# The two-way scan layer in 1024-column chunks, one channel tile at a stage, odd states' input built by ScalarE in turned form

## Chip, cores and metric

The kernel runs on one core of a Trainium2 chip. The metric is device time in microseconds (us) of one execution of the whole program, the median of several runs. The engines are TensorE (PE, its weight loads PEld), VectorE (DVE), ScalarE (ACT), GpSimd (POOL) and SyncE (SP), which issues the DMAs.

## What is computed

Four layers run one after the other on `x` of shape (4, 128, 64, 64): sparse attention, a selective scan with 64 states, rank-one attention, and a selective scan in both directions with 16 states. The change rewrites the last one:

```python
def _mamba(xf, Win, conv_w, conv_b, Wx, Wdt, bdt, A_log, D, Wout):   # xf: (1, 16384, 128)
    u, z = split(xf @ Win.T, 2)                   # 256 inner channels each
    u = silu(causal_conv(u, conv_w, taps=4) + conv_b)
    dt, Bm, Cm = split(u @ Wx.T, [8, 16, 16])
    delta = softplus(dt @ Wdt.T + bdt)
    A = -exp(A_log)                               # (256, 16)
    h[l] = exp(delta[l] * A) * h[l-1] + delta[l] * Bm[l] * u[l]    # for each of 256 x 16
    y[l] = sum_n h[l, :, n] * Cm[l, n] + u[l] * D
    return (y * silu(z)) @ Wout.T
y = _mamba(x) + flip(_mamba(flip(x)))             # both directions over 16384 positions
out = silu(group_norm(y, 4 groups)) + x
```

## The kernel before

`network` calls the four layers in turn; `xp` holds `x` with three columns of padding on both sides in SBUF, through all four. Layer 3, `two_way_scan_layer`, is the one that the change touches. It has 256 channels, two tiles (e = 0, 1) of 128, and 16 states (n), so 32 units for each chunk of `CH` = 512 columns. There are 32 chunks forward (d = 0) and 32 backward (d = 1). Each engine runs `chunks(engine, body)`: hardware loops over two chunks, with the work of a chunk K and the preparation of chunk K+1 woven in by constant positions (`N_BC`, `N_DELTA`, n or s). There is no scheduler: an engine's order is the order of the code, and semaphores tie the engines together.

For one unit s = 2n + e of chunk K: PE copies the row of B to all partitions (`broadcasts`, L1415, once for both e, a bfloat16 product with one-hot rows on three-part split values); DVE multiplies it with `du` = delta*u (`state_input`, L1623, into PSUM); ACT makes `decay` = exp(delta*A) (`decays`, L1523) and before it saves the last column of an old state (L1522, `carry`); DVE runs the recurrence (`scan`, L1631); POOL multiplies the state with C, whose row a DMA has spread over the partitions (L1573, `c_row`); PE adds the product into `y_sum` with the identity (`add_state`, L1423). The preparation of a chunk: four convolution taps folded into the input weights (`prep_u`, L1378), `prep_z` (L1387), B, C and dt (`prep_bc`, L1394), delta (`prep_delta`, L1406), softplus in steps on ACT (L1504 to L1510) and DVE (`soft_a` to `soft_d`, L1600 to L1614), the bfloat16 splits on ACT and DVE (L1587, L1593), `input_rate` on POOL (L1563). Its result: `gating` on DVE (L1639, L1643), `project` (L1430), `result` (L1649, L1652, L1654). A last part normalises and adds `x` (L1760, L1789) in eight pieces of 2048 columns.

Layer 1, `scan_layer`, is not changed, but it is a second, differently built scan in the same profile. It takes 1024 columns at a time and its states in pairs P: an even state gets its input as above (broadcast L642, product on DVE L1004); for the odd one ACT scales 128x128 blocks of the transposed `du` by a column of B (`odd_input`, L810), and PE turns them back into PSUM (`turn_back`, L652), from where the scan reads. The other lines there are `decays` L797, `scan` L1017, `keep` L1023, `product` L906 on POOL, `add_state` L662, `soft_round` L975 and `soft_max` L979 on DVE.

## Time and profile before

| | us |
|---|---|
| median of 3 runs | 11610.69 (11608.76 to 11611.1) |
| the profiled execution, own time | 11606.67 |
| its span | 11604.9 |
| layer 1, first input product to the last scans | 2986 to 6177 |
| layer 3, first input product to the last scan | 7213 to 11536 |
| layer 3, last part (affine, silu, skip) | 11553 to 11605 |

The page gives busy time by engine for the whole program, a mean of four layers with different limits. So a layer is read by a view of its own stretch: the busy time and granted TensorE clock of a window, then the timeline of single instructions inside. Where two instructions of an engine follow without idle time, start minus start is what one costs its engine; the duration of one is a little longer, since the next starts before it ends.

### The profile page before, as it was taken

To read this page: it belongs to the slowest core of one execution; us is meant where nothing else is said; L and a number is where in the kernel's file an instruction comes from. 1 tells how busy PE (TensorE), PEld (TensorE's weight loads), DVE (VectorE), ACT (ScalarE), POOL (GpSimd) and SP (SyncE) were. 2 spreads that over 40 slices of the span, in tenths; PEclk is the share of its full clock that TensorE was granted. 3 is DMA by queue.
4 is the path that set the end of the run, shared out by engine and by line. 5 is a ranking of instruction groups with operands and counts; after the bars stand their busy time and mean duration, and the time that the engine had idled before them with its cause. 6 is when DMAs were issued, how large, how long until landed. Compare 5 with 4: busy or idle time off the path is not lost. (4 is left out here: it accounts for less than half of the span.)

```text
span 11604.9 us, 133673 instructions
## 1 busy us (share of the span) xinstructions
PE 10299.4 (89%) x37124; PEld 5447.6 (47%) x37124; DVE 9629.0 (83%) x10210; ACT 7224.1 (62%) x13486; POOL 5495.9 (47%) x3348
## 2 busy tenths in 40 slices
PE   9999999999899999999999999778778777777775
PEld 6767777677444444444444454333333333322332
DVE  6858668587799999999993122999999999999998
ACT  5636556365688888888885545555555555555554
POOL 0000000000578888887882000666666666666665
PEclk9999989899899999999999999888888888898897
DMA  0000000000355455455451000222222222222223
GB/s 37 0 1 0 0 0 0 0 0 0 128 169 170 171 168 171 169 171 170 170 175 48 0 0 13 67 66 69 67 66 67 69 69 70 72 70 69 70 72 112
DMA packets 317319, 872.87 MB, mean 75 GB/s; under 512 B 35985, under 2 KB 36113, under 8 KB 314257
## 3 DMA queue, kind: packets, MB, share of 16 engines
q1 hardware_dynamic: 316912, 868.43, 23.0%
q8 instruction: 136, 2.23, 0.1%
q14 instruction: 271, 2.21, 0.1%
HBM read 834.73 MB, written 33.55 MB: 75 GB/s over the span
## 5 line engine op out<-in xcount | busy, mean ns | idle before, releaser
L1573 POOL TENSOR_TENSOR l_ring<-l_ring 128x512 f32<-128x512 f32 x2048 | 2678.6, 1329 | 1332.8 <-DVE l_ring L1631 818.1
L906 POOL TENSOR_TENSOR l_hc<-l_h,l_hc 128x1024 f32<-128x1024 f32 x1024 | 2412.1, 2377 | 613.8 <-DVE l_h L1017 613.3
L1423 PE MATMUL l_ps<-l_ring,w_sb 128*128 128x512 f32 x4096 | 2273.8, 681 | 371.8 <-DVE l_gated L1639 308.7
L1631 DVE TENSOR_TENSOR_SCAN l_ring<-l_ring,l_carry,l_ps 128x512 f32<-128x512 f32 x2048 | 2524.9, 1263 | 0.0
L662 PE MATMUL l_ps<-l_hc,w_sb 128*128 128x512 f32 x4096 | 1947.3, 597 | 32.7 <-POOL l_hc L906 27.0
L1017 DVE TENSOR_TENSOR_SCAN l_h<-l_decay,l_carry,l_ps 128x1024 f32<-128x1024 f32 x768 | 1759.3, 2332 | 3.7 <-PE l_ps L652 0.2
L1523 ACT ACTIVATE l_ring<-l_delta,w_sb 128x512 f32<-128x512 f32 x2048 | 1444.8, 708 | 48.4 <-DVE l_ring L1631 33.0
L1423 PEld LDWEIGHTS l_ps<-l_ring,w_sb 128*128 128x128 f32 x4096 | 845.8, 213 | 1224.1 <-issue 983.9
L114 POOL COPY l_qm<-l_q 128x128 f32 x128 | 82.3, 645 | 2728.2 <-PE l_ps L175 2331.0
L797 ACT ACTIVATE l_decay<-l_delta,w_sb 128x1024 f32<-128x1024 f32 x1024 | 1161.6, 1139 | 285.5 <-DVE l_h L1017 284.3
L1623 DVE TENSOR_TENSOR l_ps<-l_du,l_ps 128x512 f32<-128x512 f32 x2048 | 1299.4, 678 | 27.3 <-DVE l_ring L1631 18.4
L810 ACT ACTIVATE l_xt<-l_duT,l_BT 128x128 f32<-128x128 f32 x4096 | 1246.1, 387 | 0.0
L199 PE MATMUL l_ps<-l_attnT,l_vT 128*128 128x128 f32 x8192 | 1112.5, 279 | 1.7 <-ACT l_attnT L267 1.7
L175 PE MATMUL l_ps<-l_k,l_qm 128*128 128x512 f32 x2048 | 1023.9, 603 | 25.0 <-DVE l_E L370 18.9
L662 PEld LDWEIGHTS l_ps<-l_hc,w_sb 128*128 128x128 f32 x4096 | 741.4, 191 | 624.9 <-issue 498.8
L199 PEld LDWEIGHTS l_ps<-l_attnT,l_vT 128*128 128x128 f32 x8192 | 994.6, 192 | 47.0 <-ACT l_attnT L267 43.2
L1522 ACT ACTIVATE l_carry<-l_ring 128x1 f32<-128x1 f32 x1984 | 376.6, 190 | 1025.0 <-DVE l_delta L1614 778.0
L1415 PE MATMUL l_ps<-l_stack,sel 96*128 96x512 bf16 x1024 | 415.5, 406 | 576.8 <-DVE l_ps L1623 573.7
L1159 PE MATMUL l_ps<-l_E,l_hs 128*128 128x512 f32 x2048 | 880.0, 592 | 5.2 <-DVE l_hs L1225 5.2
L376 DVE SCALAR_TENSOR_TENSOR l_E<-l_relu,l_E 128x1024 f32<-128x1024 f32 x512 | 626.3, 1224 | 287.4 <-ACT l_E L260 287.4
L260 ACT ACTIVATE l_E<-l_E,l_offsets 128x1024 f32<-128x1024 f32 x512 | 587.0, 1147 | 290.8 <-DVE l_E L370 290.8
L370 DVE TENSOR_TENSOR l_E<-l_relu,l_ps 128x1024 f32<-128x1024 f32 x512 | 624.9, 1221 | 138.8 <-ACT l_relu L254 138.2
(222 smaller groups left out, 13282.6 us busy)
## 6 DMA issues: line engine op xcount, KB each, us to landing
l_hc<-l_rows_dram SPq DMA_DIRECT2D x1024, 512.0 KB, 3.7
l_ring<-l_rows_dram SPq DMA_DIRECT2D x1024, 256.0 KB, 3.2
l_recon_dram<-l_recon SPq DMA_DIRECT2D x64, 256.0 KB, 3.4
l_loaded<-l_recon_dram SPq DMA_DIRECT2D x32, 256.0 KB, 3.5
l_ring<-l_recon_dram SPq DMA_DIRECT2D x8, 1024.0 KB, 7.0
out<-l_ring SPq DMA_DIRECT2D x8, 1024.0 KB, 4.9
xp<-x_in SPq DMA_DIRECT2D x1, 6144.0 KB, 23.8
l_rows_dram<-l_z SPq DMA_DIRECT2D x16, 256.0 KB, 4.4
```

Source lines behind the costliest of these rows:

```text
L175: ins = nc.tensor.matmul(logits[c % 2][:, j * BANK:(j + 1) * BANK], qm[:, h, :], k[:, c * CH + j * BANK:c * CH + (j + 1) * BANK], start=Tr ...
L199: ins = nc.tensor.matmul(ps[:, 7 - h, 0:128], vT[:, t * 128:(t + 1) * 128], attnT[:, g % 2, j * 128:(j + 1) * 128], start=t == 0, stop=t = ...
L662: ins = nc.tensor.matmul(y_sum[:, half(j)], ident, hc[:, unit % CS, half(j)], start=q == 0, stop=q == S1 - 1)
L797: nc.scalar.activation(decay[:, unit % DS, :], delta[:, p, :], ACT.Exp, scale=wt("A")[:, q:q + 1]).then_inc(decay_ready, 1)
L810: ins = nc.scalar.activation(xt[:, (2 * P + hf) % XS, t * 128:(t + 1) * 128], duT[:, p, blk, :], ACT.Identity, scale=BT[:, p, blk, k:k + 1])
L906: nc.gpsimd.tensor_tensor(hc[:, unit % CS, :], h[:, unit % HS, :], hc[:, unit % CS, :], ALU.mult).then_inc(hc_done, 1)
L1017: nc.vector.tensor_tensor_scan(h[:, unit % HS, :], decay[:, unit % DS, :], odd_in if odd else even_in, before, ALU.mult, ALU.add).then_inc ...
L1423: nc.tensor.matmul(y_sum[:, e, :], ident, hc[:, (n * TI + e) % 4, :], start=n == 0, stop=n == S3 - 1).then_inc(sum_mm, 1)
L1523: nc.scalar.activation(decay[:, s % DS, :], delta[:, p, e, :], ACT.Exp, scale=col("A", e * S3 + n)).then_inc(decay_ready, 1)
L1573: nc.gpsimd.tensor_tensor(hc[:, s % 4, :], h[:, s % DS, :], c_row[:, n % CS, :], ALU.mult)\
L1623: nc.vector.tensor_tensor(x_in[:, s % 2, :], du[:, p, s % TI, :], b_psum[:, s // TI % 2, :], ALU.mult)\
L1631: nc.vector.tensor_tensor_scan(h[:, s % DS, order], decay[:, s % DS, order], x_in[:, s % 2, order], carry[:, s:s + 1], ALU.mult, ALU.add). ...
```

## The change

Layer 3 is rewritten after the pattern of layer 1. Chunks have 1024 columns, 16 forward and 16 backward. A *stage* S is one chunk K and one channel tile e: 64 stages with 16 states in 8 pairs r = 0 to 7, 512 pairs P in all. The code of all stages is written out, without hardware loops. The even state's input stays on PE and DVE (`broadcast_B`, `even_input`); the odd state's is made by ACT (`odd_input`, eight instructions) and turned back by PE (`turn_back`, eight transposes), for which PE transposes `du` (`turn_du`) and the odd rows of B (`turn_B`). The saved column of a state goes from ACT to DVE (`keep`, two small copies for a pair). POOL takes two steps of softplus, the gating, and both subtractions of the split. z and the gate are computed in the forward direction alone, kept in DRAM (`gate_dram`), and loaded in the backward one. `x` is stored to DRAM by layer 2 and loaded in windows `xw`; so the last part loads `x` too. The C rows are loaded straight into the slots `hc`, five of them, and multiplied in place. The weights of layer 3 are loaded at its start, not during layer 2. Semaphores of layer 0 are cleared and used again.

```diff
 def rank_one_attention_layer(...):
         def _(sp):
-            for to, at, signal in loads:
-                sp.dma_start(to, at).then_inc(signal, 16)
+            for b in range(B):
+                for j in range(0, NB, 2):
+                    sp.wait_ge(bank_free, NB + b * NB + j + 2)
+                    at = slice(b * N + j * BANK, b * N + (j + 2) * BANK)
+                    sp.dma_start(x_dram[:, at], x[:, at]).then_inc(x_stored, 16)
...
 def two_way_scan_layer(...):
-    CH = BANK
+    CH = 1024
...
 @block.tensor
+            def turn_back(P):
+                at_least(pe, scan_done, 2 * P)
+                for hf in range(2):
+                    pe.wait_ge(xt_ready, 2 * P + hf + 1)
+                    for t in range(4):
+                        ins = nc.tensor.transpose(odd_bank(hf)[:, t * 128:(t + 1) * 128],
+                                                  xt[:, (2 * P + hf) % XS, t * 128:(t + 1) * 128], ident)
+                    ins.then_inc(xt_mm, 1)
+            def pieces(S, r):
+                    if r == 0 and more:
+                        for j in range(2):
+                            project_delta(S + 1, j)
+                    if r == 1 and e == 1 and K + 1 < NK:
+                        turn_B(K + 1)
+                    if r in (1, 2) and n < 4 * NK:
+                        conv(n, [2 * r - 2, 2 * r - 1])
+                    if r == 2 and forward(K):
+                        project_z(S, 0)
+                    if r in (3, 4) and n < 4 * NK:
+                        conv(n + 1, [2 * r - 6, 2 * r - 5])
+                    if r == 4 and forward(K):
+                        project_z(S, 1)
+                    if r == 5 and more:
+                        turn_du(S + 1, 0)
+                        turn_du(S + 1, 1)
+                    if r in (6, 7) and e == 0 and K + 1 < NK:
+                        project_bc(K + 1, r - 6)
+                    if r in (6, 7) and e == 1 and K:
+                        project_out(K - 1, r - 6)
+                for P in range(NS * PAIRS):
+                    turn_back(P)
+                    if P:
+                        add_state(2 * P - 2)
+                    pieces(*divmod(P, PAIRS))
+                    if P + 1 < NS * PAIRS:
+                        broadcast_B(P + 1)
+                    if P:
+                        add_state(2 * P - 1)
...
 @block.scalar
+            def pieces(S, r):
+                    if r == 0 and more:
+                        for j in range(2):
+                            delta_copy(S + 1, j)
+                    if r == 1 and more:
+                        soft_exp(S + 1)
+                    if r == 2 and forward(K):
+                        silu_u(n)
+                        silu_z(S, 0)
+                        exp_set()
+                    if r == 4 and forward(K):
+                        silu_u(n + 1)
+                        silu_z(S, 1)
+                        exp_set()
+                for P in range(NS * PAIRS):
+                        decays(2 * P + 2)
+                        odd_input(P + 1)
+                        decays(2 * P + 3)
+                    pieces(*divmod(P, PAIRS))
...
 @block.gpsimd
+                for P in range(NS * PAIRS):
+                    product(2 * P)
+                    product(2 * P + 1)
+                    if r == 1 and S:
+                        gating(S - 1)
+                    if S % TI == 1 and S // TI + 1 < NK:
+                        if r == 1:
+                            split_rest(S // TI + 1)
+                        if r == 5:
+                            split_last(S // TI + 1)
+                    if S + 1 < NS:
+                        if r == 2:
+                            soft_low(S + 1)
+                        if r == 3:
+                            soft_sum(S + 1)
+                        if r == 4:
+                            input_rate(S + 1)
...
 @block.vector
+                for P in range(NS * PAIRS):
+                    scan(P, 0)
+                    scan(P, 1)
+                    if r == 0 and S:
+                        add_y(S - 1)
+                    if P + 1 < NS * PAIRS:
+                        even_input(P + 1)
+                    if S // TI % NCH < NCH - 1:
+                        keep(2 * P)
+                        keep(2 * P + 1)
+                    pieces(S, r)
...
 @block.sync
             def _(sp):
+                def load(i):
+                    sp.dma_start(buf[:, i % 2, :], recon_dram[:, at]).then_inc(buf_in[i % 2], 16)
+                    sp.dma_start(skip[:, i % 2, :], x_dram[:, at]).then_inc(buf_in[i % 2], 16)
```

On PE, in the loop over chunks, before: a broadcast and two state sums for two 512-column units (one n, both tiles), then a tap.

```order
2949 L1378 MATMUL l_ps<-xp,l_taps 128x512
2950 L1415 MATMUL l_ps<-l_stack,sel 128x512
2951 L1422 REGISTER_ALU
2952 L1423 MATMUL l_ps<-l_ring,w_sb 128x512
2953 L1422 REGISTER_ALU
2954 L1423 MATMUL l_ps<-l_ring,w_sb 128x512
```

On PE now, in a forward stage, pairs 1 (from its `turn_B`) and 2; L1496 is `turn_back`, L1506 `add_state`, L1486 `broadcast_B`, L1435 a convolution tap, L1443 z.

```order
3541 L1456 MATMUL l_ps<-w_sb,l_rest 128x32 x8
3542 L1435 MATMUL l_ps<-l_xw,l_taps 128x512 x2
3543 L1486 MATMUL l_ps<-l_stack,sel 128x512 x2
3544 L1506 MATMUL l_ps<-l_ring,w_sb 128x512 x2
3545 L1496 MATMUL l_ps<-w_sb,l_xt 128x128 x8
3546 L1506 MATMUL l_ps<-l_ring,w_sb 128x512 x2
3547 L1435 MATMUL l_ps<-l_xw,l_taps 128x512 x2
3548 L1443 MATMUL l_ps<-l_xw,w_sb 128x512
```

What moved: every pair of states now carries eight transposes, and preparation stands in each of the eight places of a stage.

On POOL before, where `input_rate` of the next chunk (L1563) stands among the products (L1573):

```order
182 L1563 TENSOR_TENSOR l_du<-l_delta,l_u 128x1024
183 L1573 TENSOR_TENSOR l_ring<-l_ring 128x512 x4
```

On POOL now, in a stage with e = 1, pairs 1 to 5 (products are L1786; `gating` L1781, `split_rest` L1751, `soft_low` L1760, `soft_sum` L1765, `input_rate` L1771, `split_last` L1755):

```order
480 L1781 TENSOR_TENSOR l_yg<-l_yg,l_gate 128x1024
481 L1751 TENSOR_TENSOR l_rest<-l_rest,l_part 96x1024
482 L1786 TENSOR_TENSOR l_ring<-l_ring 128x1024 x2
483 L1760 TENSOR_TENSOR l_z<-l_z 128x1024
484 L1786 TENSOR_TENSOR l_ring<-l_ring 128x1024 x2
485 L1765 TENSOR_TENSOR l_delta<-l_delta,l_z 128x1024
486 L1786 TENSOR_TENSOR l_ring<-l_ring 128x1024 x2
487 L1771 TENSOR_TENSOR l_du<-l_delta,l_u 128x1024
488 L1786 TENSOR_TENSOR l_ring<-l_ring 128x1024 x2
489 L1755 TENSOR_TENSOR l_stack<-l_rest,l_part 96x1024
```

What moved: one extra instruction behind the two products of a pair became one in each of pairs 1 to 4, two in pair 1 of every second stage.

## Rows read from the trace of the kernel before

**Rows 1.** The page: span; busy time and share of the span by engine
```profile
span 11604.9 us, 133673 instructions
PE 10299.4 (89%) x37124; PEld 5447.6 (47%) x37124; DVE 9629.0 (83%) x10210; ACT 7224.1 (62%) x13486; POOL 5495.9 (47%) x3348
```
**Rows 2.** Windows: busy time by engine and granted clock, layer 1 and layer 3
```profile
core 0: us, PE busy (x) PEld busy (x) DVE busy (x) ACT busy (x) POOL busy (x), PEclk, DMA share, GB/s
2986.00:6177.00 3191.00, 3014.38 (x10930) 1513.78 (x10930) 3154.60 (x2562) 2588.76 (x5501) 2576.98 (x1100) 0.99 0.50 169
7213.00:11536.00 4323.00, 3378.87 (x7118) 1344.36 (x7118) 4273.93 (x4758) 2402.81 (x5100) 2822.95 (x2111) 0.88 0.23 69
```
**Rows 3.** Lines L1631, L1623: count, ns min/median/max, first and last start
```profile
L1631 DVE TENSOR_TENSOR_SCAN l_ring<-l_ring,l_carry,l_ps x2048: 1242/1266/1280, 7214.2 to 11534.6; 128x512 f32<-128x512 f32 x187
L1623 DVE TENSOR_TENSOR l_ps<-l_du,l_ps x2048: 661/680/697, 7213.0 to 11532.9; 128x512 f32<-128x512 f32 x187
```
**Rows 4.** Timeline of DVE in layer 1: start, duration, instruction, count
```profile
4598.01 4.58 DVE L1017 TENSOR_TENSOR_SCAN l_h<-l_decay,l_zero,l_ps 128x1024 f32<-128x1024 f32 x2
4602.50 1.21 DVE L1004 TENSOR_TENSOR l_ps<-l_du,l_ps 128x1024 f32<-128x1024 f32 x1
4603.62 0.21 DVE L1023 COPY l_carry<-l_h 128x1 f32<-128x1 f32 x2
4603.75 4.58 DVE L1017 TENSOR_TENSOR_SCAN l_h<-l_decay,l_zero,l_ps 128x1024 f32<-128x1024 f32 x2
```
**Rows 5.** Timeline of PE in layer 1, the same place
```profile
4600.41 0.60 PE L642 MATMUL l_ps<-l_stack,sel 96*128 96x512 bf16 x2 [1.34 <-DVE l_h L1017]
4600.85 1.88 PE L662 MATMUL l_ps<-l_hc,w_sb 128*128 128x512 f32 x4
4602.64 1.09 PE L652 MATMUL l_ps<-w_sb,l_xt 128*128 128x128 f32 x8
4603.57 1.88 PE L662 MATMUL l_ps<-l_hc,w_sb 128*128 128x512 f32 x4
4605.29 1.02 PE L618 MATMUL l_ps<-xp,l_taps 128*128 128x512 f32 x2
4606.15 0.60 PE L642 MATMUL l_ps<-l_stack,sel 96*128 96x512 bf16 x2
```
**Rows 6.** Timelines of POOL and DVE in layer 1, around its softplus steps
```profile
4607.57 9.28 POOL L906 TENSOR_TENSOR l_hc<-l_h,l_hc 128x1024 f32<-128x1024 f32 x4
...
5908.52 5.65 POOL L906 TENSOR_TENSOR l_hc<-l_h,l_hc 128x1024 f32<-128x1024 f32 x2
...
5897.15 2.00 DVE L975 TENSOR_SCALAR l_usq<-l_z 128x1024 f32<-128x1024 f32 x1
...
5910.53 1.42 DVE L979 SCALAR_TENSOR_TENSOR l_delta<-l_delta,l_z 128x1024 f32<-128x1024 f32 x1
```
**Rows 7.** Timeline of ACT in layer 1: two decays, eight odd inputs
```profile
4599.30 2.23 ACT L797 ACTIVATE l_decay<-l_delta,w_sb 128x1024 f32<-128x1024 f32 x2
4601.44 2.43 ACT L810 ACTIVATE l_xt<-l_duT,l_BT 128x128 f32<-128x128 f32 x8
```
**Rows 8.** Timeline of ACT at the start of layer 3: a table load
```profile
7204.55 1.06 ACT L1506 ACTIVATE l_z<-l_z 128x1024 f32<-128x1024 f32 x1
7205.67 1.28 ACT L1510 ACT_TABLE_LOAD   x1
```
**Rows 9.** PE in layer 3 after a wait, and the window of that stretch
```profile
8434.68 3.64 PE L1423 MATMUL l_ps<-l_ring,w_sb 128*128 128x512 f32 x4 [3.97 <-DVE l_gated L1639]
...
8434.60:8438.20 3.60, 3.52 (x5) 1.56 (x6) 3.56 (x5) 1.97 (x2) 1.27 (x1) 0.53 0.04 16
```
**Rows 10.** ACT in the last part; landing time of its 1 MB loads (page)
```profile
11554.50 4.08 ACT L1760 ACTIVATE l_ring<-l_ring,l_shift,l_scale 128x2048 f32<-128x2048 f32 x2
...
11596.14 2.09 ACT L1760 ACTIVATE l_ring<-l_ring,l_shift,l_scale 128x2048 f32<-128x2048 f32 x1 [3.00 <-DMA l_ring<-l_recon_dram]
...
l_ring<-l_recon_dram SPq DMA_DIRECT2D x8, 1024.0 KB, 7.0
```

More of the change, by code:

```diff
@@ L1325, in two_way_scan_layer, with place, keeps_before, _ @@
+        def place(K):
+            d, c = divmod(K, NCH)
+            return (NCH - 1 - c) * CH if d else c * CH
+        forward = lambda K: K < NCH
+        def keeps_before(P):
+            d, i = divmod(P, NCH * TI * PAIRS)
+            kept_pairs = (NCH - 1) * TI * PAIRS
+            return 2 * (d * kept_pairs + min(i, kept_pairs))
+        with nc.Block() as block:
+            @block.gpsimd
+            def _(pool):
+                pool.sem_clear(retired)
         with nc.Block() as block:
@@ L1493, in split_again @@
-                def split_again(K):
-                    act.wait_ge(rest_ready, K + 1)
-                    nc.scalar.activation(part[:], rest[:], ACT.Copy).then_inc(middle, 1)
-                def deltas(K, p):
-                    for e in range(TI):
-                        act.wait_ge(delta_mm, K * TI + e + 1)
-                        nc.scalar.activation(delta[:, p, e, :], [even, odd][e], ACT.Identity,
-                                             bias=col("dtr_b", e)).then_inc(delta_out, 1)
-                    act.drain()
-                    nc.scalar.activation(z1[:], delta[:, p, :, :], ACT.Abs)
-                    act.drain()
-                    nc.scalar.activation(z1[:], z1[:], ACT.Exp, scale=-1.0).then_inc(exp_ready, 1)
@@ new lines, in _ @@
+                for j in range(2):
+                    rest_copy(0, j)
+                split_high(0)
+                split_middle(0)
+                for j in range(2):
+                    delta_copy(0, j)
+                exp_set()
+                soft_exp(0)
+                soft_log(0)
+                for n in (4, 5):
+                    silu_u(n)
+                exp_set()
+                for j in range(2):
+                    duT_copy(0, j)
+                decays(0)
+                odd_input(0)
@@ new lines, in soft_round, with soft_max @@
+                def soft_round(T):
+                    dve.wait_ge(exp_ln, 2 * T + 1)
+                    nc.vector.tensor_scalar(z3[:], z1[:], 1.0, 1.0, ALU.add, ALU.subtract).then_inc(soft_steps, 1)
+                def soft_max(T):
+                    dve.wait_ge(exp_ln, 2 * T + 2)
+                    own = delta[:, T % 2, :]
+                    nc.vector.scalar_tensor_tensor(out=own, in0=own, scalar=0.0, in1=z2[:], op0=ALU.max,
+                                                   op1=ALU.add).then_inc(soft_steps, 1)
@@ new lines, in keep, with pieces @@
+                def keep(unit):
+                    S, q = divmod(unit, S3)
+                    K, e = divmod(S, TI)
+                    at = CH - 1 if forward(K) else 0
+                    dve.wait_ge(scan_done, unit + 1)
+                    nc.vector.tensor_copy(carry[:, e * S3 + q:e * S3 + q + 1], h[:, unit % HS, at:at + 1]).then_inc(kept, 1)
+                def pieces(S, r):
+                    K, e = divmod(S, TI)
+                    if e == 1 and K + 1 < NK:
+                        if r == 1:
+                            bt_copy(K + 1)
+                    if S + 1 < NS:
+                        if r == 2:
+                            soft_round(S + 1)
+                        if r == 3:
+                            soft_max(S + 1)
+                    if r in (6, 7) and e == 1 and K and not forward(K - 1):
+                        result(K - 1, r - 6)
+                    if r == 3 and S == (NCH - 2) * TI:
+                        dve.wait_ge(z_mm, 4 * (NCH - 3) + 4)
+                        nc.vector.memset(xw[:, NCH % 3, CH:CH + PAD], 0.0).then_inc(pad_ready, 1)
@@ L1707, in _ @@
[L1707 to L1709 removed]
+                bt_copy(0)
+                soft_round(0)
+                soft_max(0)
+                even_input(0)
+                for P in range(NS * PAIRS):
+                    S, r = divmod(P, PAIRS)
+                    scan(P, 0)
+                    scan(P, 1)
+                    if r == 0 and S:
+                        add_y(S - 1)
+                    if P + 1 < NS * PAIRS:
+                        even_input(P + 1)
[3 more added lines that the diff above has]
+                    pieces(S, r)
```

872 lines of the change are left out of this document (466 added, 406 removed).

## The prediction

> **What bounds the kernel now.** I read the page first: PE is busy 89% of the span, but that is a mean of four layers [rows 1]. So I take layer 3's own window next. There DVE is busy 4273.9 of 4323 us, PE 3378.9, POOL 2823.0, ACT 2402.8, at a granted clock of 0.88 [rows 2]. DVE is the bound, and waits for nobody: 2048 scans and 2048 input products lie end to end from 7213.0 to the last scan's end near 11536 [rows 3]. A 1024-column pair of states costs four times (1.18 + 0.59) = 7.1 us there; softplus, splits, gating and results make the rest.
>
> Layer 1 is the pattern that layer 3 shall follow, with the same 1024 scans of 1024 columns. It took 3191 us, again DVE bound (3154.6 busy), at clock 0.99, with PE at 94% and ACT and POOL at 81% [rows 2]. The question is whether layer 3 gets layer 1's time or is stopped by PE or POOL, which have more to prepare: a stage has 8 pairs to hide it, layer 1's chunk had 32.
>
> **Demand of each engine for a stage.** Starts minus starts:
>
> - DVE: a pair is two scans (4.49), the even product (1.12) and two copies (0.13), 5.74 in all: 4603.75 - 4598.01 [rows 4]. Eight make 45.9. To this come `soft_round` 2.00 and `soft_max` 1.42 [rows 6], `add_y` about 1.2 (one SBUF and one PSUM input, as the even product), `bt_copy`, and in the backward direction two result pieces of about 1.4 in every second stage. 50.6 us forward, some 52 backward.
> - PE: a pair is the broadcast 0.44, two state sums of 1.79 and 1.72, the eight transposes 0.93: 4.88; a 128x512 float32 product costs 0.86 (4606.15 - 4605.29) [rows 5]. Eight pairs make 39.0. Preparation of a stage: 8 taps, 2 delta products, 2 (4 in every second) of `project_bc` or `project_out`, counted per stage as 4 in two adjoining places, `turn_du` 0.93, and z twice forward. That is r0 1.72, r1 1.72, r2 2.58, r3 1.72, r4 2.58, r5 0.93, r6 and r7 1.72: 14.7 us forward, 13.0 backward, and 0.9 for `turn_B` with e = 1. So 54.2 forward and 52.5 backward: above DVE. The delta product, with 8 rows, is counted like the others.
> - POOL: a product is 2.33 us (9.28 for four) [rows 6]. Sixteen, the three softplus and rate steps and the gating make 46.6; with e = 1 the two subtractions of the split make 51.3, if they cost 2.33 too. No row has a bfloat16 input on POOL; I bound them by half and twice the product, 1.2 and 4.7, and take the product's value since the count of columns is the same.
> - ACT: a pair is two decays 2.14 and the odd input 2.34 or so [rows 7], 4.5 in all, 36 for a stage. Forward preparation is ten activations of 0.6 to 1.06 and four table loads of 1.28 (5.1): 14.5, and 2.1 more for the splits: 50.3 and 52.5 us. Backward it is two loads and no z: 47.
>
> The table load has its own row: the activation before it ends at 7205.61, the load starts at 7205.67 and is over 1.28 later [rows 8]. The Trainium skill (ScalarE: Activation LUTs, What ACT_TABLE_LOAD costs) gives 1.283 us and a drain of 1.38 for every switch. By that a forward stage of ACT would be 56 to 58 us and about 60 us would be added over 32 stages. The trace shows no drain here; I stay with the row.
>
> **The path in a stage.** All four engines lie within 10% of each other, so the order decides. In r6, r7 and r0 PE is last: 4.88 + 1.72 = 6.6 each. In r0 `add_y` waits for the last state sum, at the end of PE's place. It is done 1.3 us into r1; the first state sum of the new stage waits half a microsecond for it; then DVE makes the even product and the first scan, which ends 4.9 us into r1. From there **POOL** has one chain without a gap: pairs 1 to 4 hold 8 products and 4 preparation steps, 12 operations of 2.33 = 28.0, with e = 1 13 operations = 30.3. Its last is `input_rate`, and the very next place, r5, has `turn_du` on PE waiting for it. One product in that stretch is held up by `soft_max`: two took 5.65 instead of 4.67 beside it [rows 6], so +1.0. After it PE has the transposes 0.93, the broadcast 0.44 and a state sum 1.72: 3.1.
>
> Stage = 6.6 + 4.9 + 28.0 + 1.0 + 3.1 + 2 x 6.6 = **56.8 us**, with e = 1 **59.1**. Against it PE alone has 54.2 or less: PE stands 2 to 5 us at r5. Queued behind that wait are the broadcast for pair 6 and a state sum, so DVE waits too; nobody else has work to fill it. ACT, a pair ahead, isn't late anywhere in this sum, though in r2 to r4 forward only by about a microsecond.
>
> A wait of 3.97 us before L1423 was followed by 3.6 us at half clock: four records took 3.47 instead of 1.72 [rows 9]. The waits of layer 1 end at 2.3 us or so, and its clock was 0.99. With e = 1 the wait is 3.5 to 5 us, so I add 2.0 to these stages. Mean (56.8 + 61.1)/2 = 58.9; 64 stages = **3772 us**, against 4323.
>
> **Around the loop.** Ahead: layer 2's last store, then 1.3 MB of weights and the first window, which no longer load under layer 2; 1 MB lands in 7.0 us [rows 10]. The first chunk's preparation is twice as wide. Before, it took from 7181 to 7213, 32 us. I take +29 (bounds +15 and +60, the whole preparation doubled and the loads in a row). The drain of the last stage has 1024-wide steps: +6 (0 to 12). The last part moved 16.8 MB in 41.6 us for seven of eight pieces, ACT waiting for the loads [rows 10]; half as much again for `x` is +25 (0 if latency set it, 30). Stores of x, z and recon lie beside work, on SP's queue between C loads, which have some 4 us in hand: POOL reaches a product 8 us after PE frees its slot, and a C row lands in about 4. If that cover fails, a product waits and the POOL chain grows by as much; nothing in the trace lets me exclude 1 us a stage. Reused semaphores cost one short block. Layers 0 to 2 don't change.
>
> Sum: 11606.7 - 4323 + 3772 + 60 = 11115.4; the profiled execution lies 4 below the median: **11120 us**, ratio 0.958.
>
> **Rivals.**
>
> 1. *PE alone sets the end.* POOL catches up (split steps at 1.2, `soft_max` harmless, gating early). Then a stage is PE's 54.2 or 52.5 and 0.6 for the `add_y` wait, 53.9: 11120 - 64 x 5.0 = 10800. For it: POOL's demand is below PE's. Against: the twelve operations in a row, at 2.33, can't be shortened by anything in the code.
> 2. *More waits, or the clock.* The clock stays at the 0.88 of layer 3 before [rows 2], since PE again waits once or twice a stage. PE's 53.4 become 60.7, with 3 us of POOL wait left 63.7: 64 x 63.7 = 4077, 11425. Hops between engines that I set at nothing lead to the same side: 0.1 us in each of 24 is 2.4 a stage, 11270. For it: all engines tie. Against: layer 1 held 0.99 at the same share of PE. The Trainium skill (TensorE: Matmul & The Clock Gate, Part 4: PE-mode transpose) says that transposes don't count as PE activity for the clock; the change adds over seventy to a stage. By that rule the clock would sink as in this rival. The trace disagrees: layer 1's pairs have the same eight transposes and ran at 0.99 [rows 2, 5].
> 3. *Slower.* One mechanism: half clock lasts. It decides when a stage exceeds (4323 - 60)/64 = 66.6 us, that is a mean clock under 53.4/66.6 = 0.80 on PE. At 0.75 a stage is 71.2: 11606.7 - 4323 + 4557 + 60 = 11901. Before, with PE only 78% busy, it was still 0.88, which speaks against.
> 4. *It isn't done as said*: layer 3 stays DVE bound, as layer 1: 50.6 to 52 us a stage, 3285, 10630. PE's demand excludes it, unless products are cheaper than 0.86.
>
> **Numbers.** My sum, stages of 56 to 60.5 us (10930 to 11220): 0.55. Rival 1: 0.12. Rival 2, 11220 to 11500: 0.26. Rival 3: 0.04. Rival 4: 0.03. The range goes from 10880 (stage 55.2) to 11360 (62.7), which leaves out most of rivals 1, 3 and 4 and the end of 2. A measurement tells 0.2% (23 us) from no change. Faster 0.95, within 0.2% 0.01, slower 0.04.
>
> **What would show it.** DVE in layer 3 idle for some 8 us a stage, most of it before the even product and behind PE. PE waiting for `du` from POOL once a stage, 2 to 3 us with e = 0 and 4 to 5 with e = 1, and at half clock just after the latter. POOL without a gap from pair 1 to pair 4. Forward and backward stages alike (if backward is 1.7 us shorter, PE set it). The last part near 77 us instead of 52. I am wrong if PE waits for ACT's copies of the two preparation banks, if POOL waits for C rows, or if the POOL chain has gaps.

## The result, and the profile of the changed kernel

The changed kernel takes **11139.74 us** (11137.64 to 11143.06, four runs) beside 11610.9 (11608.76 to 11612.1): ratio 0.9594, 95% interval 0.9579 to 0.961. The forecast was 11120 us. The profiled execution has a span of 11139.1 us, 465.8 less than the 11604.9 of before.

The page of the changed kernel, span and busy time by engine, answering to [rows 1]:

```profile
span 11139.1 us, 128149 instructions
PE 10416.8 (94%) x41860; PEld 5841.7 (52%) x41860; DVE 8778.3 (79%) x8226; ACT 7929.4 (71%) x14477; POOL 5817.0 (52%) x2580
```

Windows of layer 3's loop, whole, forward and backward (columns as in [rows 2]: window, its us, busy time and count of PE, PEld, DVE, ACT, POOL, granted clock, DMA share, GB/s):

```profile
7245.00:11055.00 3810.00, 3479.34 (x11808) 1729.84 (x11806) 3416.17 (x2775) 3098.46 (x6074) 3131.29 (x1337) 0.98 0.48 161
...
7245.00:9150.00 1905.00, 1769.55 (x5999) 878.18 (x5998) 1697.24 (x1360) 1629.44 (x3136) 1561.36 (x670) 0.98 0.47 158
9150.00:11055.00 1905.00, 1709.79 (x5810) 851.65 (x5808) 1718.93 (x1416) 1469.02 (x2939) 1569.93 (x667) 0.98 0.49 163
```

DVE was busy 99% of the layer's loop before and is busy 90% now; PE went from 78% to 91%, POOL from 65% to 82%, and the clock from 0.88 to 0.98. No engine is full. The loop, from its first even product (7238.06) to the end of its last scan (11050.85), is 3812.8 us, 59.6 us a stage. Forward and backward take nearly the same time (1909 and 1902 us from scan to scan), though PE has less to do backward: PE doesn't set the end alone.

Waits of the changed kernel between 7260 and 11000 (engine and line, what it waited for, us in total, times, longest):

```profile
POOL l_ring L1786 <- DVE l_ring L1868: 588.1, 222, 4.9
DVE l_ps L1852 <- PE l_ps L1486: 247.8, 203, 4.2
...
PE l_ps L1469 <- POOL l_du L1771: 147.2, 63, 2.7
...
DVE l_yg L1836 <- PE l_ps L1506: 131.2, 62, 2.6
```

The third row is the wait that the forecast put in pair 5: once in each stage, 2.3 us on average. In the same stretch POOL waits for no DMA, and PE for nothing of ACT's. One whole stage with e = 1 shows how it comes about. Timeline of POOL (start, duration, line, operation; in brackets the idle time before it and what ended it):

```profile
8140.19 4.69 POOL L1786 TENSOR_TENSOR l_ring<-l_ring 128x1024 f32<-128x1024 f32 x2 [4.93 <-DVE l_ring L1868]
8144.83 2.38 POOL L1781 TENSOR_TENSOR l_yg<-l_yg,l_gate 128x1024 f32<-128x1024 f32 x1
8147.15 2.15 POOL L1751 TENSOR_TENSOR l_rest<-l_rest,l_part 96x1024 f32<-96x1024 f32 x1
8149.24 4.68 POOL L1786 TENSOR_TENSOR l_ring<-l_ring 128x1024 f32<-128x1024 f32 x2
8154.56 2.34 POOL L1760 TENSOR_TENSOR l_z<-l_z 128x1024 f32<-128x1024 f32 x1 [0.63 <-DVE l_z L1823]
8156.88 4.69 POOL L1786 TENSOR_TENSOR l_ring<-l_ring 128x1024 f32<-128x1024 f32 x2
8162.73 2.35 POOL L1765 TENSOR_TENSOR l_delta<-l_delta,l_z 128x1024 f32<-128x1024 f32 x1 [1.16 <-DVE l_delta L1828]
8165.05 4.68 POOL L1786 TENSOR_TENSOR l_ring<-l_ring 128x1024 f32<-128x1024 f32 x2
8169.69 2.35 POOL L1771 TENSOR_TENSOR l_du<-l_delta,l_u 128x1024 f32<-128x1024 f32 x1
```

Thirteen operations from the first scan of the new stage to du, and two gaps (0.63 and 1.16), each ended by one of DVE's softplus steps. The timeline of DVE at the same place:

```profile
8135.24 1.28 DVE L1836 SCALAR_TENSOR_TENSOR l_yg<-l_u,w_sb,l_ps 128x1024 f32<-128x1024 f32 x1 [2.56 <-PE l_ps L1506]
...
8150.14 4.34 DVE L1823 TENSOR_SCALAR l_z<-l_z 128x1024 f32<-128x1024 f32 x1
8154.40 4.57 DVE L1868 TENSOR_TENSOR_SCAN l_ring<-l_ring,l_carry,l_ps 128x1024 f32<-128x1024 f32 x2
8158.89 1.20 DVE L1852 TENSOR_TENSOR l_ps<-l_du,l_ps 128x1024 f32<-128x1024 f32 x1
...
8160.13 2.52 DVE L1828 SCALAR_TENSOR_TENSOR l_delta<-l_delta,l_z 128x1024 f32<-128x1024 f32 x1
```

`soft_round` (L1823) starts at 8150.14, while POOL is in a pair of products that ends at 8153.92, and ends 0.56 after them; alone it takes 0.68. Over the 64 stages (min/median/max in ns):

```profile
L1823 DVE TENSOR_SCALAR l_z<-l_z x64: 682/2922/5190, 7227.3 to 10967.8; 128x1024 f32<-128x1024 f32 x64
...
L1828 DVE SCALAR_TENSOR_TENSOR l_delta<-l_delta,l_z x64: 2161/2512/3111, 7228.4 to 10974.4; 128x1024 f32<-128x1024 f32 x64
```

Last, PE in the same stage, at its waits:

```profile
8112.30 1.06 PE L1469 MATMUL l_ps<-w_sb,l_du 128*128 128x128 f32 x8 [2.17 <-POOL l_du L1771]
...
8136.58 1.98 PE L1506 MATMUL l_ps<-l_ring,w_sb 128*128 128x512 f32 x4 [0.50 <-DVE l_yg L1836]
...
8156.79 0.60 PE L1486 MATMUL l_ps<-l_stack,sel 96*128 96x512 bf16 x2 [1.42 <-DVE l_ring L1868]
...
8172.18 1.06 PE L1469 MATMUL l_ps<-w_sb,l_du 128*128 128x128 f32 x8 [2.17 <-POOL l_du L1771]
8173.08 0.72 PE L1486 MATMUL l_ps<-l_stack,sel 96*128 96x512 bf16 x2
8173.60 3.49 PE L1506 MATMUL l_ps<-l_ring,w_sb 128*128 128x512 f32 x4
```

After the wait at 8172 four records of state sums take 3.33 us (8173.60 to 8176.93, where `turn_back` follows) instead of 1.72: half clock, that is 1.2 instead of 2.4 GHz. After the equal wait at 8112 they don't.

### The profile page after: what moved, and what is told of

Read it like the earlier page. It is cut to its first block and busy times, and to the rows that moved or that the text cites. A ratio compares the mean times of both kernels' runs of the same rounds, so it can differ in the third digit from the quotient of the medians.

```text
span 11139.1 us, 128149 instructions
## 1 busy us (share of the span) xinstructions
PE 10416.8 (94%) x41860; PEld 5841.7 (52%) x41860; DVE 8778.3 (79%) x8226; ACT 7929.4 (71%) x14477; POOL 5817.0 (52%) x2580
## 5 line engine op out<-in xcount | busy, mean ns | idle before, releaser
L1786 POOL TENSOR_TENSOR l_ring<-l_ring 128x1024 f32<-128x1024 f32 x1024 | 2429.0, 2394 | 609.6 <-DVE l_ring L1868 608.2
L1868 DVE TENSOR_TENSOR_SCAN l_ring<-l_ring,l_carry,l_ps 128x1024 f32<-128x1024 f32 x960 | 2200.5, 2332 | 7.1 <-PE l_ps L1496 5.9
L1506 PE MATMUL l_ps<-l_ring,w_sb 128*128 128x512 f32 x4096 | 1983.5, 607 | 86.7 <-POOL l_ring L1786 55.1
L1663 ACT ACTIVATE l_ring<-l_delta,w_sb 128x1024 f32<-128x1024 f32 x1024 | 1164.5, 1139 | 190.6 <-DVE l_ring L1868 189.5
L1676 ACT ACTIVATE l_xt<-l_duT,l_BT 128x128 f32<-128x128 f32 x4096 | 1246.0, 388 | 0.0
L811 ACT ACTIVATE l_xt<-l_duT,l_BT 128x128 f32<-128x128 f32 x4096 | 1246.0, 387 | 0.0
L1506 PEld LDWEIGHTS l_ps<-l_ring,w_sb 128*128 128x128 f32 x4096 | 755.3, 194 | 714.7 <-issue 518.3
L1852 DVE TENSOR_TENSOR l_ps<-l_du,l_ps 128x1024 f32<-128x1024 f32 x512 | 623.2, 1217 | 258.1 <-PE l_ps L1486 257.8
L1192 ACT ACTIVATE l_E<-l_g,l_neg_max,l_f 128x4096 f32<-128x4096 f32 x128 | 486.4, 3800 | 379.0 <-PE l_ps L1165 367.1
L254 ACT ACTIVATE l_relu<-l_ps,l_offsets 128x1024 f32<-128x1024 f32 x512 | 570.2, 1114 | 234.8 <-PE l_ps L175 233.0
```

Of the source, the lines that this page charges most:

```text
L811: ins = nc.scalar.activation(xt[:, (2 * P + hf) % XS, t * 128:(t + 1) * 128], duT[:, p, blk, :], ACT.Identity, scale=BT[:, p, blk, k:k + 1])
L1506: ins = nc.tensor.matmul(y_sum[:, half(j)], ident, hc[:, unit % CS, half(j)], start=q == 0, stop=q == S3 - 1)
L1663: nc.scalar.activation(decay[:, unit % DS, :], delta[:, S % 2, :], ACT.Exp, scale=col("A", S % TI * S3 + q)).then_inc(decay_ready, 1)
L1676: ins = nc.scalar.activation(xt[:, (2 * P + hf) % XS, t * 128:(t + 1) * 128], duT[:, S % 2, 4 * hf + t, :], ACT.Identity, scale=BT[:, K % ...
L1786: nc.gpsimd.tensor_tensor(hc[:, unit % CS, :], h[:, unit % HS, :], hc[:, unit % CS, :], ALU.mult).then_inc(hc_done, 1)
L1868: nc.vector.tensor_tensor_scan(h[:, unit % HS, order], decay[:, unit % DS, order], x_now[:, order], before, ALU.mult, ALU.add).then_inc(sc ...
```

## The experiments

All are made from the changed kernel, whose time is taken as 11139.7 us throughout. Ratios are to the kernel before, whose median beside them was 11608.2 to 11611.7 us.

### What lies on TensorE's path

**proj1** takes 0.86 us of PE out of each of pairs 6 and 7; **taps2** takes 3.4 us out of pairs 1 to 4.

```diff
# proj1, in project_bc and in project_out
-                    for e in range(TI):
+                    for e in range(1):
...
# taps2, in conv
                     for k in some:
+                        if k in (1, 2):
+                            continue
```

> The two projections of pairs 6 and 7 contract only the first of the two channel tiles (the second tile's products are left out, so their sums are not the reference's): TensorE has 0.86 us less in each of pairs 6 and 7 of every stage, 1.72 us in a stage, 110 us in 64 stages. Theory of the prediction (pairs 6, 7 and 0 are TensorE's path at 6.6 us each): nearly one for one, 11139 - 110 = about 11030, 11020 to 11060. Rival (VectorE's scans and the reversal of z set those pairs, TensorE only follows): under 20 us, 11120 to 11140. Between them: VectorE's scans of pairs 6 and 7 sit on TensorE's finish for half of it, about 11085.

> Two of the four convolution taps are left out, so PE has one 0.86 us product less in each of pairs 1 to 4, 3.4 us a stage. Theory (POOL's chain runs through pairs 1 to 5): what PE saves there is given back as a longer wait for du; 0 to 1 us a stage, 11080 to 11140. Rival (PE's work sets the stage): 3.4 x 64 = 220 us less, 10920.

proj1: 11026.73 us (11023.4 to 11027.51), ratio 0.9499 (0.9483 to 0.9514). 113 us for 110 us of products: nearly one for one, though some 15 us of it are the clock (a stage without half clock in it is 1.3 or 1.8 us shorter than in the changed kernel, on average 1.5, that is 97 us in 64 stages). taps2: 11137.19 us (11133.2 to 11140.91), ratio 0.9592 (0.9576 to 0.9608): nothing for 218 us of products. So pairs 6 and 7 are PE's path, and in pairs 1 to 4 PE has room; what it is given there it spends waiting. Stages without half clock are as long as in the changed kernel, 57.3 us with e = 0 and 59.9 with e = 1. In a forward window of taps2 PE is busy 1631 us of 1850 instead of 1719, at a slightly lower clock:

```profile
7250.00:9100.00 1850.00, 1631.24 (x5549) 810.51 (x5548) 1630.65 (x1326) 1571.47 (x3031) 1519.04 (x647) 0.97 0.48 158
```

### POOL's chain between them

**pool_half** halves the eight pairs of products of a stage.

```diff
-nc.gpsimd.tensor_tensor(hc[:, unit % CS, :], h[:, unit % HS, :], hc[:, unit % CS, :],
+nc.gpsimd.tensor_tensor(hc[:, unit % CS, 0:BANK], h[:, unit % HS, 0:BANK], hc[:, unit % CS, 0:BANK],
```

> Each of the eight POOL products of a stage covers 512 of the 1024 columns (the other half of h times C is left out): POOL has about 8 x 1.17 = 9.4 us less a stage and the chain to u*delta and to the input products ends well before TensorE asks for it. If POOL's chain is what the wait of TensorE for du in pair 5 (2.3 us a stage) and the later half-rate pieces rest on: those go, and VectorE's blocked rounding (2.9 to 5.2 us instead of 0.68) shortens too: a stage of 54 to 56 us, 64 x (59.6 - 55) = about 290 us less, 10800 to 10900. Rival (the wait for du is hidden behind VectorE's scans, which end a stage anyway): within 60 us of 11139.

10769.56 us (10769.24 to 10770.82), ratio 0.9277 (0.9262 to 0.9293): 370 us less, 30 us beyond the range expected. The expectation counted eight products, 9.4 us; a stage has sixteen, and each is 1.28 instead of 2.35 us, some 17 us in all. Either is more than the chain is late by. PE's wait for du is gone forward; backward about 0.95 us of it is left in 30 stages (28.6 us in all). The forward window and the rounding:

```profile
7250.00:9100.00 1850.00, 1830.51 (x6421) 930.75 (x6420) 1701.62 (x1459) 1728.83 (x3354) 1082.96 (x718) 1.00 0.53 176
```

```profile
L1823 DVE TENSOR_SCALAR l_z<-l_z x64: 682/879/1861, 7227.1 to 10601.9; 128x1024 f32<-128x1024 f32 x64
```

PE is busy 99% of a forward stage at full clock, and a stage is 53.8 us, 64 x 5.8 = 370 less than 59.6. That is what the first rival of the forecast gave for PE alone (53.9 us, 10800): the mechanism of that rival is right, and POOL is what keeps it from coming about. Of the 5.8 us the next runs give about 1.2 to the clock (fill) and 0.6 to the rounding (round_small); no run parts what is left.

**round_small** takes only the rounding off DVE.

```diff
# POOL's soft_low
-nc.gpsimd.tensor_tensor(z3[:], z1[:], z3[:], ALU.subtract).then_inc(low_ready, 1)
+nc.gpsimd.tensor_tensor(z3[:], z1[:], z2[:], ALU.subtract).then_inc(low_ready, 1)
# DVE's soft_round
-dve.wait_ge(exp_ln, 2 * T + 1)
-nc.vector.tensor_scalar(z3[:], z1[:], 1.0, 1.0, ALU.add, ALU.subtract).then_inc(soft_steps, 1)
+dve.wait_ge(exp_ln, 2 * T + 2)
+nc.vector.tensor_scalar(z3[:, 0:1], z1[:, 0:1], 1.0, 1.0, ALU.add, ALU.subtract).then_inc(soft_steps, 1)
```

> VectorE's rounding of the softplus (add 1, subtract 1) is cut to one column, and POOL's next operation subtracts another tile that is ready early instead of the rounded one: the softplus's low part is left out, the count of POOL's operations is the same. It takes 2.9 us (even stages' median) to 5.2 us off VectorE, which stands between two scans there, and POOL's 0.63 us wait for it. Theory 1 (a blocked rounding on VectorE delays the scans of its pair and POOL's chain, and with them the end of a stage): 1.0 to 1.5 us a stage, 11040 to 11075. Theory 2 (VectorE has slack in that pair, and only POOL's 0.63 us counts): 11095 to 11105. Theory 3 (neither counts): 11130 to 11140.

11100.7 us (11097.11 to 11104.61), ratio 0.9563 (0.9547 to 0.9579): 39 us, 0.61 a stage. Theory 2: it is worth about the 0.63 us for which POOL had waited, and no more. DVE's 2.9 to 5.2 us in that place had been beside the path. They don't all go either; in the stage looked at `soft_max` now stands beside POOL's products and is held up in its turn:

```profile
8150.24 0.14 DVE L1823 TENSOR_SCALAR l_z<-l_z 128x1 f32<-128x1 f32 x1
...
8157.19 4.86 DVE L1828 SCALAR_TENSOR_TENSOR l_delta<-l_delta,l_z 128x1024 f32<-128x1024 f32 x1
```

**gate_dve** moves the gating from POOL's chain to DVE, ahead of the first scan of pair 1; all of the computation is kept.

```diff
# POOL, after the first two products of a stage
-                    if r == 1 and S:
-                        gating(S - 1)
# DVE, after add_y and the even product
+                    if r == 0 and S:
+                        gating(S - 1)
...
+                    nc.vector.tensor_tensor(yg[:, S % 3, :], yg[:, S % 3, :], gate[:, e, :], ALU.mult).then_inc(gated_ready, 1)
```

> The gating product goes from POOL to DVE, behind the even product of pair 1. Everything is computed. Theory: POOL's chain loses one of 12 or 13 operations, 2.33 us, and PE's wait for du with it; but DVE gets 1.2 us just where the first scan of pair 1 is late, so net 1 to 1.5 us a stage: about 11060. Rival (PE alone): no change from 11140. Rival (DVE is nearer to the bound than its busy time says, since its softplus steps stand blocked beside POOL): slower than 11140, up to 11200.

11064.3 us (11062.42 to 11071.4), ratio 0.9528 (0.9512 to 0.9543): 75 us, as expected. POOL's chain loses 2.33 us and starts 1.1 later, by the gating on DVE:

```profile
8127.01 1.22 DVE L1811 TENSOR_TENSOR l_yg<-l_yg,l_gate 128x1024 f32<-128x1024 f32 x1
8128.14 4.58 DVE L1865 TENSOR_TENSOR_SCAN l_ring<-l_ring,l_carry,l_ps 128x1024 f32<-128x1024 f32 x2
```

With e = 1 the chain from its first product to du is 29.5 us instead of 31.85, which leaves 1.2 us of gain. With e = 0 POOL catches up with the next pair's scan and waits 1.06 us for it, so that nothing is left there. Half of the gain, then, is the chain (0.6 us a stage); the other half comes with the clock, which is 0.99 instead of 0.98: 75 us of the loop are at half clock instead of 154. The wait for du is 2.17 in nearly all stages, and 2.7 in none.

### The wait and the clock

The changed kernel's trace shows the price of half clock in its stages. Taken from one turning of du to the next, a stage with e = 0 lasts 57.3 us when no half clock falls in it and 59.0 to 59.7 when it does, one with e = 1 lasts 59.9 and 61.3 to 61.6. The first stage here (9132.88 to 9190.25) has none, the second (9190.25 to 9251.84) has it at its start; the last two rows show a place where the clock is already at half, 0.50, in the wait before the first transpose:

```profile
9132.88 1.07 PE L1469 MATMUL l_ps<-w_sb,l_du 128*128 128x128 f32 x8 [2.17 <-POOL l_du L1771]
9190.25 1.63 PE L1469 MATMUL l_ps<-w_sb,l_du 128*128 128x128 f32 x8 [2.73 <-POOL l_du L1771]
9251.84 1.77 PE L1469 MATMUL l_ps<-w_sb,l_du 128*128 128x128 f32 x8 [2.19 <-POOL l_du L1771]
...
8709.84 1.94 PE L1469 MATMUL l_ps<-w_sb,l_du 128*128 128x128 f32 x8 [2.72 <-POOL l_du L1771]
```

```profile
8709.35:8709.80 0.45, 0.00 (x0) 0.00 (x0) 0.00 (x0) 0.00 (x0) 0.45 (x2) 0.50 0.25 82
```

In the trace's record of the granted clock it falls to half at 40 of 61 such waits (25 of the 31 in stages with e = 1, 15 of the 30 with e = 0), though the waits with e = 1 are the shorter ones. What decides it is not shown.

**fill** keeps the wait, and gives PE something to do in it.

```diff
# PE, pair 5, ahead of turn_du
+                        for fill in range(2):
+                            nc.tensor.matmul(V, ident, w[:, 0:BANK], start=True, stop=True)
                         turn_du(S + 1, 0)
```

> All of the computation is kept; ahead of the wait for du in pair 5, TensorE multiplies two constant tiles into the bank that du's transposes then overwrite: two products of 512 columns, 1.72 us at full clock, in a place where it idles 2.3 us a stage anyway. It tells the wait apart from what follows it. The granted clock is 0.98 in the loop, so 4% of a stage of 59.6 us, 2.4 us, go at 1.2 GHz, and cost 1.2 us a stage against full clock. Theory (the 1.2 GHz stretches follow from TensorE's idle 2.2 to 2.7 us before du, and their price is on the path): with the gap filled the clock stands at 1.00, and 64 x 1.2 = 77 us come back: 11055 to 11090. Rival 1 (the low clock follows from something else, such as the waits for VectorE's scans in the same stage, or its price is hidden): clock 0.98 still, 11130 to 11150. Rival 2 (du is in time more often than the sum of the waits suggests, so the added products delay): slower, up to 11180.

11064.74 us (11063.26 to 11066.02), ratio 0.953 (0.9516 to 0.9545): with 126 useless products in it the kernel is **75 us faster** than without, 77 expected. The stretch of PE and the window of 3500 us of fill, and the same window of the changed kernel after them:

```profile
8155.22 1.88 PE L1551 MATMUL l_ps<-w_sb 128*128 128x512 f32 x4
8157.46 1.09 PE L1469 MATMUL l_ps<-w_sb,l_du 128*128 128x128 f32 x8 [0.37 <-POOL l_du L1773]
8158.39 0.60 PE L1486 MATMUL l_ps<-l_stack,sel 96*128 96x512 bf16 x2
8158.83 1.88 PE L1506 MATMUL l_ps<-l_ring,w_sb 128*128 128x512 f32 x4
```

```profile
7260.00:10760.00 3500.00, 3308.95 (x11363) 1638.59 (x11361) 3195.40 (x2621) 2923.07 (x5720) 2940.76 (x1256) 1.00 0.48 164
```

```profile
7260.00:10760.00 3500.00, 3207.01 (x10887) 1596.82 (x10887) 3133.20 (x2563) 2868.75 (x5602) 2878.34 (x1231) 0.98 0.48 161
```

PE still stands 0.37 us, and 0.93 in most stages with e = 0, and the granted clock of the window is 1.00: 2 stretches at half clock are left in the loop, of 42. Stages last 57.3 and 59.8 us, as those of the changed kernel without half clock, so the products themselves cost nothing. So the low clock follows from the wait for du, and not from the shorter waits elsewhere in a stage, and its price, 1.2 us a stage, is on the path. The Trainium skill (TensorE: Matmul & The Clock Gate, Part 4: PE-mode transpose) has it that transposes don't count as activity for the clock. The drop begins between 0.6 us ahead of the first of du's eight transposes, which follow the wait, and 1.4 us behind it; in 10 of the 40 places it begins in the wait itself, so there it isn't the transposes that bring it, and fill has the same transposes at full clock. But no run here puts other products in their place, so this trace neither confirms nor refutes the rule for them.

**du_later** takes the wait away: du is transposed in pair 6, and the two halves of a projection go to pairs 5 and 7. All of the computation is kept.

```diff
# PE, pieces
-                        turn_du(S + 1, 0)
...
+                    j = {5: 0, 7: 1}.get(r)
...
+                    if j is not None and e == 0 and K + 1 < NK:
+                        project_bc(K + 1, j)
+                    if j is not None and e == 1 and K:
+                        project_out(K - 1, j)
+                    if r == 6 and more:
+                        turn_du(S + 1, 0)
```

> turn_du (PE) and its copies (ACT) stand one place later, in pair 6 instead of 5; the halves of project_bc and project_out stand in pairs 5 and 7. Everything is computed. Theory (POOL's chain to input_rate ends last at turn_du): the 2.2 to 2.7 us that PE waited for du at each stage, and the half clock behind it, go; PE then has 54 us a stage, DVE's late softplus steps keep it at 55.5 to 56.5: 200 to 260 us less than the changed kernel, 10880 to 10940, about 10920. Rival (PE's work and hops between engines set the stage, the wait for du only shows where the lateness is collected): the wait moves to another place, and it stays within 40 us of 11140.

10957.2 us (10953.05 to 10959.21), ratio 0.9435 (0.9419 to 0.9451): 182 us less; it stays 17 us above the upper end of what was expected. By fill, 75 us of it are the clock; the rest, 107 us, is the wait itself, 1.7 of its 2.3 us a stage. PE goes through pairs 5 and 6 without standing:

```profile
8135.11 1.88 PE L1475 MATMUL l_ps<-l_yg,w_sb 128*128 128x512 f32 x4
...
8141.57 1.04 PE L1469 MATMUL l_ps<-w_sb,l_du 128*128 128x128 f32 x8
...
8146.43 1.98 PE L1506 MATMUL l_ps<-l_ring,w_sb 128*128 128x512 f32 x4 [0.79 <-POOL l_ring L1791]
```

Of the 0.6 us that don't come back, a part reappears as short waits of PE for a product that POOL brings late, of which the last row is one: in the loop they go from 54.2 to 70.0 us, and the waits for a scan ahead of the broadcast from 92.5 to 101.4.

### Work that should cost nothing, and the last part

**no_tables** turns the silu of u and the gate into plain copies, so that no table is loaded in the loop; **no_skip_load** leaves the second load of a piece out of the last part.

```diff
# no_tables; the gate's silu likewise, and the table set is loaded once
-nc.scalar.activation(u[:, K % 2, e, half(j)], [U, V][j], ACT.Silu, bias=col("conv_b", e)).then_inc(u_out, 1)
+nc.scalar.activation(u[:, K % 2, e, half(j)], [U, V][j], ACT.Identity, bias=col("conv_b", e)).then_inc(u_out, 1)
...
# no_skip_load
-sp.dma_start(skip[:, i % 2, :], x_dram[:, at]).then_inc(buf_in[i % 2], 16)
...
```

> ScalarE's silu of u and of the gate becomes a plain copy with bias, in the same number of instructions, so that one activation table serves the whole scan (the silu itself is left out, the numbers are not the reference's): the four table loads of 1.28 us of a forward stage, 5.1 us of ScalarE, are gone, 164 us in 32 forward stages. Theory of the prediction (ScalarE, busy 0.88 of a forward stage, is not on the path in the pairs where its tables change): no more than 10 us, 11130 to 11145. Rival (a table load stands ahead of a copy or an odd input that TensorE or VectorE is waiting for): each load counts for 0.3 to 1.3 us on the path of its pair, 40 to 160 us, 10980 to 11100.

> The last part doesn't load x again from DRAM; VectorE adds the tile itself instead (the skip connection is left out, the numbers are not the reference's). A piece then moves 2 MB instead of 3 MB, as in the kernel before, whose last part was 41.6 us long up to its eighth piece against 52.3 us in the changed kernel. Theory (the last part goes at the speed of its DMA): 10.7 us less, 11129, 11126 to 11132. Rival (the order of loads and stores on SP sets it): within 3 us of 11139.7.

no_tables: 11139.25 us (11135.19 to 11148.06), ratio 0.9596 (0.9581 to 0.9611). 186 table loads are gone from the loop, 128 of them forward; ACT is busy 1420 instead of 1581 us of the same forward window, and nothing moves:

```profile
7250.00:9100.00 1850.00, 1718.99 (x5837) 855.21 (x5836) 1647.69 (x1336) 1420.12 (x2925) 1514.56 (x650) 0.98 0.47 159
```

no_skip_load: 11129.25 us (11120.45 to 11129.62), ratio 0.9584 (0.9571 to 0.9597): 10.5 us, 10.7 expected. Its runs spread by 9 us, so the trace is the better witness: from the first silu to the end it is 50.5 us instead of 61.0. The last two of the eight silus of the last part, in the changed kernel and then in no_skip_load:

```profile
11122.87 2.09 ACT L1970 ACTIVATE l_ring<-l_ring,l_small 128x2048 f32<-128x2048 f32 x1 [5.39 <-DMA l_ring<-x_dram]
11130.37 2.09 ACT L1970 ACTIVATE l_ring<-l_ring,l_small 128x2048 f32<-128x2048 f32 x1 [5.41 <-DMA l_ring<-x_dram]
```

```profile
11104.60 2.09 ACT L1969 ACTIVATE l_ring<-l_ring,l_small 128x2048 f32<-128x2048 f32 x1 [4.70 <-DMA l_ring<-l_recon_dram]
11109.68 2.09 ACT L1969 ACTIVATE l_ring<-l_ring,l_small 128x2048 f32<-128x2048 f32 x1 [2.99 <-DMA l_ring<-l_recon_dram]
```

### Two faster versions

**both** is du_later and gate_dve together. **round_act** is both, with the rounding done on ACT by two additions; all of the computation is kept.

```diff
# round_act against both; minus holds -1.0
+                    nc.scalar.activation(z3[:], z1[:], ACT.Identity, bias=1.0)
+                    act.drain()
+                    nc.scalar.activation(z3[:], z3[:], ACT.Identity, bias=minus[:]).then_inc(soft_steps, 1)
...
-                    nc.vector.tensor_scalar(z3[:], z1[:], 1.0, 1.0, ALU.add, ALU.subtract).then_inc(soft_steps, 1)
```

> Both: turn_du one place later and gating on DVE. If POOL's chain was all that stood over PE's work, the second edit brings nothing any more and its 1.2 us on DVE is hidden or costs up to 1 us a stage: 10900 to 10990. If POOL is still the last one with turn_du in pair 6, another 60 to 100 us below du_later.

> On top of the version with du turned in pair 6 and the gating on VectorE (10923.95 us), the softplus's rounding is done by ScalarE as two additions, of 1 and of -1, with all of the computation kept: VectorE is without its 2.9 to 5.2 us, ScalarE has 2 more operations of about 1.1 us a stage, and its end stands before the l of POOL's chain. If VectorE sets the stage there: 64 x 1.0 to 2.5 us, 10765 to 10860, about 10830. If TensorE sets it (its busy time was 0.93 to 0.95 of the stage at full clock): 10900 to 10930. If ScalarE's drain and its two added operations delay its copies of sums: slower, 10930 to 10990.

both: 10923.95 us (10920.31 to 10926.67), ratio 0.9406 (0.939 to 0.9422), as expected; without the wait for du the gating is worth 33 us instead of 75. round_act: **10888.64 us** (10887.11 to 10889.64), ratio 0.938 (0.9364 to 0.9395), 35 us less than both. That lies between the two cases: I had taken the rounding's place on DVE for the bound (10765 to 10860), and it is worth 0.55 us a stage, about what round_small showed for the changed kernel. Its forward window:

```profile
7250.00:9100.00 1850.00, 1793.95 (x6232) 899.37 (x6231) 1719.01 (x1415) 1745.48 (x3319) 1534.89 (x662) 1.00 0.51 170
```

PE is busy 97% of it, 119 us from what pool_half shows for PE alone. This is the fastest full version.

## Why the forecast was right, point by point

Time and mechanism were right; 20 us were missing. In the profiled execution the loop is 41 us longer and what lies around it 16 shorter than in the sum, so that two errors of opposite sign partly cancel, which is luck; the profiled execution also lies 1 us above the median and not 4 below. With the profiled execution, loop -510.2, ahead of it +25.0, behind it +19.4: -465.8 in all. The forecast had -551 and +60.

- **The bound moved off DVE** as said: 10% idle, 6 us a stage, where 8 were forecast. The difference is that DVE's blocked steps count as busy (2.0 us more than forecast in the medians of `soft_round` and `soft_max`).
- **The path in a stage**, e = 1, with the rows above. From du's transposes to `add_y`: 8135.24 - 8112.30 = 22.94 (22.9 forecast). To POOL's first product: 4.95 (4.9). To the next du's transposes: 8172.18 - 8140.19 = 31.99 (31.3). In all 59.9 instead of 59.1; with e = 0 the last step is 29.4 to 29.9 instead of 29.0. Where no half clock adds to them, stages last 59.9 and 57.3 us, against 59.1 and 56.8 forecast. proj1, taps2 and pool_half show that these are the pieces that count.
- **The term mis-sized there** is "one chain without a gap" and the +1.0 for a product held up. Forward, the products aren't held up (4.68 for two); POOL waits 0.63 and 1.16 for DVE's steps instead, 1.79 in all. The split's subtractions cost 2.14 us, not 2.33, which takes 0.2 back. Together that is some 0.8 us in the stages looked at; over the whole loop 0.6, 41 us with the clock in it. In 22 stages, every backward one with e = 0 among them, there is no gap, and a pair of products takes 5.12 us and another 5.65, as in [rows 6]. The forecast had named gaps in POOL's chain as a sign that it was wrong; they are there, but they are 1.8 us of 32, and the chain stays what PE waits for.
- **soft_round** was taken at the 2.00 us of [rows 6]; it is 0.68 to 5.19, median 2.92. **soft_max**: 1.42 forecast, 2.51 measured. That they cost more didn't count on DVE (round_small), only through POOL's gaps.
- **The wait for du** is there in every stage, 2.2 to 2.7 us; 2 to 3 with e = 0 was right, 4 to 5 with e = 1 was not. It is PE's room in pairs 1 to 4, and that is smaller with e = 1 than I counted: PE itself waits there, 1.42 us before the broadcast at 8156.79, for a scan that the blocked step holds up.
- **The clock.** I added 2.0 us to stages with e = 1 because a wait of 3.5 to 5 us would bring half clock. The size was nearly right, 1.2 us a stage (fill) instead of 1.0, the reason only half: the waits are shorter than that, and half clock follows some waits of 2.17 us and not others, with e = 0 too. So that the size fits is partly luck. That it comes more often with e = 1 was right (25 of 31 waits against 15 of 30). That the waits of layer 1, up to about 2.3 us, were harmless was no bound.
- **ACT's cover** for its table loads held: no_tables shows 0.5 us for the 164 us of table loads forward and 74 backward.
- **Around the loop.** Ahead +25.0 (29 forecast), of which 4.9 come from layers 0 to 2. The forecast left them unchanged, though layer 2 now stores `x`; they end at 7186.2, and between 7184.2 and 7189.5 in the variants, 7181.3 before. The cause stays open. The drain from the last scan to the first silu grew from 18.6 to 27.3, +8.7 (6 forecast). The last part grew by 10.7, not 25: this is the term that is furthest off. A piece of 3 MB takes 7.44 us, 423 GB/s, where I had scaled the 353 of before. At 2 MB a piece it moved less in a second, and no_skip_load's pieces alternate between 5.0 and 6.8 us. The Trainium skill (Perfetto Trace Analysis, Roofline) puts a single core's ceiling at about 435 GB/s from its 16 DMA engines; by it a piece would take 7.2 us, an estimate from that page's figure, and the trace agrees within 3%.
- **The rivals.** Backward stages are no shorter than forward ones, which speaks against the first; its 53.9 us is what remains once POOL's chain is short (pool_half). The clock of 0.88 and the lasting half clock didn't come. Hops of 0.1 us on 24 steps (the 11270 case) would be 2.4 us a stage; the three sums above leave 0.8. The layer didn't stay DVE bound either (10% idle). C rows were in time: POOL waited for no DMA.

## What to carry to other kernels

Write a stage down as one chain through all engines, with start-to-start times from a layer that already has the pattern; busy shares of 81 to 91% on four engines hid a chain that was exact to 1 us in 60. Ask of every step that one engine waits for where it stands in the order of its own engine, and how much later the consumer could ask for it: moving du's transposes by one pair was worth 182 us, and halving PE's filter in the slack pairs nothing. Where PE waits for something in every stage, as for 2.3 us here, useless products in the gap can pay: they cost nothing there and kept the clock. Taking the wait away paid more (182 us against 75).

## What the runs showed of the hardware

**An operation on DVE that is held up by POOL can wait out more than one of its operations.** `soft_round` takes 0.68 us when POOL is idle; beside two products it took 4.34 us, from 0.9 us into the first to just past the end of the second. With products of half the length its median is 0.88. The Trainium skill (SBUF — State Buffer, Who interferes with whom) states that the port pair shared by VectorE and GpSimd is locked for a whole instruction and that the loser is blocked until it is free; the trace agrees that it is blocked, and its times fit a second instruction of POOL, queued right behind the first, going ahead of the waiting one.

**Half clock came with waits of 2.2 to 2.7 us**, at 40 of 61 of them, in some stages and not in others that look the same (8112 and 8172 above). It lasted 3 to 4 us, in three stages twice that, and made a stage some 1.7 us longer. Products without a use, 1.72 us of them in each stage, removed nearly all of it.

**Loads and stores together moved 423 GB/s** in the last part, at 3 MB a piece, against 353 at 2 MB in the kernel before.
